# Two mixture-of-experts stages: results scattered back per expert, weights loaded during the layernorm, a rewritten routing chain

## What is computed

```python
x = x + attn_a(layernorm(x))
x = x + ffn(layernorm(x))
x = x + attn_b(layernorm(x))
x = x + ffn(layernorm(x))

# ffn: E = 8 experts, capacity C = 2048 / 8 = 256 tokens each
logits = einsum('gtd,de->gte', xt, router_w)
probs = softmax(logits); gate = max(probs); idx = argmax(probs)
emask = one_hot(idx, E)
pos = cumsum(emask, axis=1) * emask - 1          # place of the token within its expert
dispatch = emask[..., None] * one_hot(pos, C)    # a token past the capacity is dropped
h = relu(einsum('gecd,edf->gecf', expert_inputs, w1) + b1)   # 128 -> 512
y = einsum('gecf,efd->gecd', h, w2) + b2                     # 512 -> 128
out = einsum('gecd,gtec->gtd', y, dispatch * gate)
```

## Time and profile before

| | |
|---|---|
| median of 3 runs | 1302.0 us (1299.88 to 1302.25) |
| the profiled execution, its own time | 1302.2 us |
| its span, first to last instruction | 1300.6 us |
| mean granted TensorE clock | 0.884 |
| busy: PE, weight load, DVE, ACT, POOL | 79%, 51%, 60%, 46%, 26% |
| first expert stage, statistics to last addition | 607.8 to 720.8 us |
| second expert stage, same | 1183.1 to 1293.1 us |

### The profile page before, as it was taken

How to read it: one execution, slowest core, us unless ns; L and a number is a source line. 1 busy time by engine, 2 the same in 40 slices (tenths; PEclk the granted TensorE clock), 3 DMA queues, 4 the chain that set the end, 5 groups by cost and what they waited for, 6 DMA issues and landing times. The chain is left out here.

```text
span 1300.6 us, 19242 instructions
## 1 busy us (share of the span) xinstructions
PE 1033.4 (79%) x6462; PEld 661.4 (51%) x6462; DVE 782.7 (60%) x1948; ACT 596.9 (46%) x1155; POOL 341.5 (26%) x451
## 2 busy tenths in 40 slices
PE   3499999999999999997263427879999999985180
PEld 2357666666666666664253326445544445434080
DVE  5166756766676657775212696787777777736031
ACT  2366656666666656663020300542555555563020
POOL 0421112111211022100324100773443334320504
PEclk9589999999999999998577756877999999996595
DMA  5500000000000000000142000000000000000252
GB/s 177 131 1 2 1 1 1 1 1 1 1 1 1 1 1 2 1 1 1 58 129 81 7 0 1 1 1 1 1 2 1 1 2 1 1 1 1 85 153 69
DMA packets 40028, 30.05 MB, mean 23 GB/s; under 512 B 9200, under 2 KB 35584, under 8 KB 39936
## 3 DMA queue, kind: packets, MB, share of 16 engines
q1 hardware_dynamic: 35392, 19.43, 5.4%
q0 software_dynamic: 2816, 6.30, 1.6%
q10 hardware_dynamic: 1728, 3.15, 0.8%
HBM read 21.50 MB, written 9.46 MB: 24 GB/s over the span
## 5 line engine op out<-in xcount | busy, mean ns | idle before, releaser
L709 DVE TENSOR_REDUCE attn_b_least<-attn_b_slot 128x1 f32<-128x512 f32 (+3 forms) x384 | 195.1, 553 | 62.2 <-PE attn_b_slot L627 42.0
L440 ACT ACTIVATE attn_a_prob<-attn_a_score,attn_a_m_all 128x128 f32<-128x128 f32 (+7 forms) x256 | 189.1, 739 | 74.6 <-DVE attn_a_m_all L362 70.3
L776 ACT ACTIVATE attn_b_probT<-attn_b_st 128x1024 f32<-128x1024 f32 (+1 forms) x192 | 145.2, 808 | 149.9 <-PE attn_b_st L651 148.6
L358 DVE TENSOR_REDUCE attn_a_m_far<-attn_a_score 128x1 f32<-128x512 f32 (+3 forms) x192 | 105.8, 551 | 95.3 <-PE attn_a_score L272 91.3
L296 PE MATMUL attn_a_o<-attn_a_ptsb,Vd 128*64 128x512 f32 x288 | 156.1, 624 | 0.0
L296 PE MATMUL attn_a_o<-attn_a_ptsa,Vd 128*64 128x512 f32 x288 | 156.0, 624 | 0.0
L284 PE MATMUL attn_a_slot<-tab,attn_a_prob 128*128 128x128 f32 x1152 | 150.2, 274 | 0.0
L625 PE MATMUL attn_b_slot<-KS,attn_b_alone 128*128 128x512 f32 (+2 forms) x384 | 145.8, 448 | 4.5 <-POOL attn_b_alone L798 2.9
L284 PEld LDWEIGHTS attn_a_slot<-tab,attn_a_prob 128*128 128x128 f32 x1152 | 133.1, 142 | 11.1 <-issue 2.4
L625 PEld LDWEIGHTS attn_b_slot<-KS,attn_b_alone 128*128 128x128 f32 x384 | 73.6, 202 | 87.7 <-DVE attn_b_least L709 52.6
L449 ACT ACTIVATE attn_a_ptsa<-attn_a_slot 128x512 f32<-128x512 f32 x144 | 85.7, 595 | 60.9 <-PE attn_a_slot L284 60.4
(11 more groups left out here) (219 smaller groups left out, 1926.2 us busy)
## 6 DMA issues: line engine op xcount, KB each, us to landing
moe_experts_w<-in_L_ffn_w_dram SPq DMA_DIRECT2D x20, 256.0 KB, 2.8
moe_experts_w<-in_L_ffn_w_dram ACTq DMA_DIRECT2D x12, 256.0 KB, 3.6
bias_by_query_and_key<-bias_by_distance SPq DMA_DIRECT2D x2, 1024.0 KB
bias_near<-bias_by_query_and_key SPq DMA_DIRECT2D x2, 1024.0 KB, 8.2
moe_experts_xe<-to_experts POOLq DMA_DIRECT2D x16, 128.0 KB, 2.7
from_experts<-moe_experts_ye SPq DMA_DIRECT2D x16, 128.0 KB, 3.3
to_experts<-xn SPq DMA_DIRECT2D x1, 1024.0 KB, 5.4
from_experts<-xn SPq DMA_DIRECT2D x1, 1024.0 KB, 8.9
```

Source lines behind the costliest of these rows:

```text
L358: nc.vector.tensor_reduce(least, score[t % 2][:, 0:nk - win], AX.X, ALU.min).then_inc(far_done, 1)
L440: nc.scalar.activation(probs(g)[:, j, 0:nk], score[t % 2][:, 0:nk], ACT.Exp, bias=m_all[:, j:j + 1], scale=-1.0, accum_out=rowsum[g % 2][: ...
L709: nc.vector.tensor_reduce(least[m // PER % 2][:, c, a, qt:qt + 1], bank[u % SLOTS_S][:, 0:w], AX.X, ALU.min).then_inc(slot_free, 1)
L776: nc.scalar.activation(probT[n % 2][:, two, lo:], st[:, two, lo:], ACT.Exp, scale=-1.0).then_inc(exp_done, 1)
```

## The change

- `layernorm`: the router products of four tiles are issued between the turns, after the turns of the next four. `xn` gets a row of 132 numbers (`DW = D + 4`), of which number 128 holds the token's own index.
- `moe` opens the weights of all eight experts (`w1`, `w2`, `b2`: 36 KB a partition) before the layernorm, and SP issues their 24 loads in the layernorm's block.
- `route`: the expert is picked from the shifted logits, not from the exponentials; the gate is computed later in the chain; the eight scans become one over 128 elements that reads PSUM directly, with `fresh` set to zero where a new expert begins; several pairs of operations become one, and several links are gone. One more small operation writes the token's index into `xn`.
- `experts`: the scatter of `xn` carries the index along (rows of 528 bytes). SP, not POOL, loads each expert's rows, all eight at once, into their own places. After each expert's output POOL scatters its 256 rows straight to their token's row in the second DRAM buffer (two indirect transfers of 128 rows, with the indices that came with the input rows). When all have landed, SP loads the rows back in token order with four plain transfers of 256 KB. The output buffer `ye` (a ring of two) is written again only when its two scatters have landed (`returned`). Loops are unrolled. ACT copies expert 1 before the relu of expert 0; DVE does relu(e+1) before the output addition of e.
- The buffers exist once for each `moe` call, so four are cleared beside the first attention, not two. The first block gets one more DVE operation behind its last ones, and one memset in a wait.

```diff
 # layernorm, PE
+            def logits(g):
+                pe.wait_ge(copied, g + 1)
+                for i in range(g * BLK, (g + 1) * BLK):
+                    at = 1 + (i % QT) * P
+                    nc.tensor.matmul(logit[:, i, :], xnT[:, i // QT, at:at + P], router[:, :], start=True, stop=True)
             for i in range(TILES):
                 pe.wait_ge(xn_ready, i + 1)
                 j = i % BLK
-                ins = nc.tensor.transpose(bank[i // BLK][:, j * P:(j + 1) * P], xn[:, i, :], ident[:, :])
+                ins = nc.tensor.transpose(bank[i // BLK][:, j * P:(j + 1) * P], xn[:, i, 0:D], ident[:, :])
                 if j == BLK - 1:
                     ins.then_inc(turned, 1)
-            for i in range(TILES if router is not None else 0):
-                ...
+                    if router is not None and i >= BLK:
+                        logits(i // BLK - 1)
+            if router is not None:
+                logits(TILES // BLK - 1)
 # route, DVE
-            nc.vector.memset(one[:, :], 1.0)
+            nc.vector.memset(fresh[:, :, :], 1.0)
             link(nc.vector.tensor_reduce(m1[:, :], logit[:, :, :], AX.X, ALU.max))
-            ... L949 to L978
+            nc.vector.tensor_tensor(rank[:, :, :], logit[:, :, :], wide(m1), ALU.subtract).then_inc(shifted, 1)
+            nc.vector.tensor_scalar(token, spare[:, :], -(SLOTS + 1.0), None, ALU.add)
+            dve.wait_ge(shifted, 1)
+            link(nc.vector.scalar_tensor_tensor(best[:, :, :], rank[:, :, :], 0.0, prio[:, :, :], ALU.is_equal, ALU.mult))
+            link(nc.vector.tensor_reduce(m2[:, :], best[:, :, :], AX.X, ALU.max))
+            nc.vector.tensor_tensor(mask_bf[:, :, :], best[:, :, :], wide(m2), ALU.is_equal).then_inc(masked, 1)
+            nc.vector.tensor_tensor(mask[:, :, :], best[:, :, :], wide(m2), ALU.is_equal)
+            link(nc.vector.memset(fresh[:, :, 0:1], 0.0))
+            link(nc.vector.tensor_tensor(base[:, :, :], mask[:, :, :], ebase[:, :, :], ALU.mult))
+            link(nc.vector.tensor_reduce(first_row[:, :], base[:, :, :], AX.X, ALU.add))
+            link(nc.vector.tensor_tensor(first_row[:, :], first_row[:, :], spare[:, :], ALU.subtract))
+            dve.wait_ge(exped, 1)
+            nc.vector.tensor_reduce(m3[:, :], ex[:, :, :], AX.X, ALU.max)
+            link(nc.vector.tensor_reduce(m4[:, :], ex[:, :, :], AX.X, ALU.add))
+            link(nc.vector.reciprocal(m5[:, :], m4[:, :]))
+            nc.vector.tensor_tensor(gate[:, :], m3[:, :], m5[:, :], ALU.mult)
+            dve.wait_ge(counted, 1)
+            link(nc.vector.tensor_tensor_scan(run[:, :, :].rearrange("p e t -> p (e t)"), fresh[:, :, :].rearrange("p e t -> p (e t)"),
+                                              total, 0.0, ALU.mult, ALU.add))
+            dve.wait_ge(counted, 2)
+            ... subtract total, add count, times mask, sum, keep, row, times keep
+            nc.vector.scalar_tensor_tensor(slot[:, :], row[:, :], -1.0, spare[:, :], ALU.add, ALU.add)
 # experts, POOL after the scatters of xn
-            pool.wait_ge(sent, 16 * TILES)
-            ... rows of each expert, then the 16 gathers
+            for e in range(E):
+                pool.wait_ge(ye_ready, e + 1)
+                for c in range(2):
+                    token = xe[:, 2 * e + c, D:D + 1].bitcast(I32)
+                    pool.indirect_dma_start(out=ye_dram[:, :], out_offset=bass.IndirectOffsetOnAxis(ap=token, axis=0),
+                                            in_=ye[e % RING][:, c, :], in_offset=None).then_inc(returned[e % RING], 16)
 # experts, SP
+            sp.wait_ge(sent, 16 * TILES)
+            for e in range(E):
+                sp.dma_start(xe[:, 2 * e:2 * e + 2, :], bass.AP(tensor=xe_dram, offset=e * (CAP * DW),
+                                                                ap=[[DW, P], [P * DW, 2], [1, DW]])).then_inc(xe_ready[e], 16)
+            for i in range(RING):
+                sp.wait_ge(returned[i], 32 * (E // RING))
+            for i in range(TILES // BLK):
+                sp.dma_start(back[:, i * BLK:(i + 1) * BLK, :], bass.AP(tensor=ye_dram, offset=i * (BLK * P * D),
+                                                                       ap=[[D, P], [P * D, BLK], [1, D]])).then_inc(fetched[i], 16)
 # experts, ACT and DVE
+            copy(0)
+            copy(1)
+            relu(0)
+            for e in range(E):
+                if e + 1 < E:
+                    relu(e + 1)
+                if e + 2 < E:
+                    copy(e + 2)
 ...
+            relu(0)
+            for e in range(E):
+                if e + 1 < E:
+                    relu(e + 1)
+                dve.wait_ge(y_done, e + 1)
+                if e >= RING:
+                    dve.wait_ge(returned[e % RING], 32 * (e // RING))
+                nc.vector.tensor_tensor(ye[e % RING][:, :, :], y_ps[e % RING][:, :, :],
+                                        b2[:, e, :].unsqueeze(1).to_broadcast([P, 2, D]), ALU.add).then_inc(ye_ready, 1)
 # build, moe: SP, in the layernorm's block
+                        for e in range(E):
+                            sp.dma_start(w1[:, e, :], t["w1"][e]).then_inc(weights[e], 16)
+                            sp.dma_start(w2[:, e, :, :], t["w2"][e].rearrange("(f p) d -> p f d", p=P)).then_inc(weights[e], 16)
+                            sp.dma_start(b2[:, e, :], row(t["b2"], D, e * D)).then_inc(weights[e], 16)
 # build, first block, DVE, between the two bf16 copies
+            nc.vector.tensor_scalar(xn[:, :, D].bitcast(I32), col["spare"], -1.0, None, ALU.add)
```

More of the change, by code:

```diff
@@ L1150, in _, with relu @@
-            with dve.Fori(0, ITS) as it:
-                body(it)
+            def relu(e):
+                dve.wait_ge(h_done, 2 * e + 2)
+                if e >= RING:
+                    dve.wait_ge(y_done, e - RING + 1)
+                for f in range(2, FB):
+                    ins = nc.vector.tensor_scalar(hT[e % RING][:, f, :], h_ps[2 * (e % RING) + 1][:, f % 2, :],
+                                                  b1T[:, f, e:e + 1], 0.0, ALU.add, ALU.max)
+                ins.then_inc(relu_dve, 1)
```

277 lines of the change are left out of this document (97 added, 180 removed).

## The result

The changed kernel took 1258.5 us, the median of four runs (1256.5 to 1265.3), beside 1301.5 for the kernel before (1299.9 to 1302.3). The ratio is 0.968 (95% interval 0.964 to 0.972). The forecast was 1262.3. Timed a second time, the same pair gave 1263.8 and 1298.3, ratio 0.973 (0.970 to 0.976), so the gain is 35 to 43 us and is not known more closely than that. The profiled execution took 1256.5 (span 1254.7), 45.8 less than that of before.

What follows compares the result with a forecast made beforehand. It took the expert stages to be bound by serial scatters, landings, experts and gathers, with PE stalled by ACT and DVE order. Gains of 20.25 us per stage, twice 40.5, less 0.65, took 1302.2 to 1262.3; range 1255.5 to 1272.

Steps and rivals of the forecast that it cites:

- the return: Last expert output to last rows back: 24.1 us becomes 9.8, a gain of 14.3 per stage, bounds 12.0 to 15.3.
- the routing: Routing chain after the layernorm: 9.1 us becomes 6.5, a gain of 2.6 per stage, bounds 2.0 to 3.0.
- Waits for `returned`: Expert loop: output buffer waits for scatters two experts back; costs nothing while a scatter costs POOL under about twice 1.28 us.
- The rivals in which POOL binds: Expert loop: each scatter waits for the previous landing, 2.53 us each, 11.8 more per stage, 1286 us; chance 0.08.
- the slower one: Expert loop: scatters dearer than 3.04 us each make the kernel slower than before; at 3.3 and 0.3, 1320 us; chance 0.02.
- Order on ACT and DVE: Expert loop: copy(1) before relu(0) and relu(7) before ye(6) remove two PE stalls, 2.85 us per stage, bounds 2.0 to 2.9.
- Rows: Last scatter's landing to PE's first turn: 2.86 us becomes 2.35 with SP loading, a gain of 0.5 per stage.
- Router products: Layernorm: moving products between turns gains 0, as PE has no idle time there; bounds 3 us either way.
- Weights beside the layernorm: Layernorm block: SP's 24 weight issues take 11.6 us and end before PE's last product, costing 0.
- a sign of being wrong: Layernorm block: the forecast would be wrong if SP's last weight issue ended a layernorm block.
- the rival: Layernorm block: SP's weight issues hold its end, price 2.5 us, giving 1264.8; chance 0.13.
- Once: Costs once per kernel: 0.5 us for SP's extra semaphore clears before the final store, 0.15 for one DVE operation.

Runs made afterwards that it cites:

- the old way back: Changed kernel with SP storing each expert's rows and POOL gathering 16 tiles at the end, as before the change: 1286.0 us, ratio 0.992.
- the products last: Changed kernel with the router products issued after all layernorm turns, as before the change: 1258.7 us, ratio 0.970.
- the unread products of the experts block: Changed kernel plus sixteen 128x128 products that nobody reads, on PE once the twelfth scatter has landed: 1256.3 us, ratio 0.968.

## Why the prediction was right, and where it was not

**The sum.** The stages gave 38.7 us where the terms gave 40.5, and the medians 43.0 and 34.5 where the forecast said 39.9. The terms were right within 1 us each but for one, the second layernorm, and the errors had both signs: what this one lost (2.7 us), and what the return lost (0.9 a stage), the loop and the routing gave back in part (0.7 and 0.5 a stage). That they cancel so nearly is luck, and so is how near a single median comes to the forecast, with stretches outside the change moving by up to 7 us. What is not luck is the return, over two thirds of the sum, with the mechanism that was forecast.

**Return: mechanism right, one piece left out.** The last output to the last rows took 10.5 and 10.4 us in the two stages; I had 9.8. Inside it the pieces moved: 0.27 instead of 0.8 from the wait to a scatter; but the last output comes 1.8 us after the one before it, since no relu stands between them any more, and its scatters queue behind that pair, so that the first starts 1.0 after the output. The landing took 2.24, as assumed, so the scatters are 0.3 over in all. The four loads took 5.9 and 5.7 us from the first issue to the last landing (5.5 to 5.9 in six stages), against 5.5 assumed, which was nearer than either row, 5.0 or 6.7. The 6.15 us that the Trainium skill (DMA: Bandwidth & Descriptors, section Bandwidth) states for 1 MB are the transfer alone, measured for one issued from GpSimd; all six stages here took less, with issue and landing included. I also ended the sum at the last rows. Behind them DVE still has 1.5 us of additions, 0.3 more than before, because from the first landing on the 16 additions leave it hardly idle. Late rows (0.6) and the longer end (0.3) are the 0.9 by which the term missed.

**Waits for `returned` and POOL.** No idle time of DVE is put down to the scatters, they stand 1.27 apart and 0.97 long beside DVE's work, and the old way back left the loop unchanged. The rivals in which POOL binds, and the slower one, did not happen. The port rule of the Trainium skill (SBUF — State Buffer, section Who interferes with whom) had no price here; DVE's operations in the loop take one input from PSUM, so the loop is no test of operations with two inputs in SBUF.

**Order on ACT and DVE: sum right, owners wrong.** The loop gave 3.5 to 3.7 instead of 2.85. The order alone is worth about 2 of it (1.8 to 2.5), most of it at the end. The step that failed is "copy(1) ahead of relu(0) removes the stall": the profile's releaser of ACT's idle time was PE's hidden layer, which neither of these two needs, and which the queued load of `w1` did. I read who held PE (ACT) and did not read what held ACT.

**Rows.** The gain was 0.44 / 0.50, as said; the first rows landed 2.23 after SP's issue.

**Routing.** 6.0 instead of 6.5 and outside its bound of 6.1. The one scan took 0.41, between the estimate 0.34 and the bound 0.6; the rest is overlap: operations that aren't linked start before the one ahead has ended (1171.43, 1171.64 and 1171.76 in a row of 0.29, 0.17 and 0.29), and two maxima and a memset cost little beside others. I had added durations; unlinked operations are to be counted by their spacing.

**Router products: in the bounds, and not zero.** The forecast had no change in either stage. PE's last product came 0.5 us sooner in the first and 2.6 later in the second. The step that failed is taking the clock of the second stage as given: the rows showed that the turns ran at half speed and the products at full, and I took that as a matter of time and not of what PE had done before. "PE has no idle time that the products could fill" was wrong as well, by 0.5 us: turns that show as gapless were waiting for DVE.

**Weights beside the layernorm.** 24 issues took 13.9 and 13.8 us, not 11.6. The six in a row that I measured were the first of their block; from the twelfth issue on, the `b2` issues, of 0.5 us, took 0.7 to 1.4. In the second stage PE's slower block hid it; with the products last SP held that block by 0.3. In the first stage SP started 2.1 us after the statistics, behind the semaphores of the attention, and ended 16.0 to 16.8 after them, not near 13; the interleaved products ended at 16.0 too. So SP's last issue ended the first layernorm's block in all three profiles of the changed kernel, which the prediction had named as a sign of being wrong, and part or all of the 0.5 us that the interleaving gains there went to it. The step that failed is the price of an issue, taken from six; the rival was right about the mechanism and had the price too high (2.5; measured 0.2 to 0.9, in one stage).

**Once.** The final store was issued 0.37 later, 0.5 forecast.

## What to carry to other kernels

A term that ends in a transfer has to be followed to the last instruction that uses the data: when a slow producer goes, more of the consumer's own work stands behind the last landing. And a chain names the transfer that released something, which need not be the last of its group. When the profile says that PE waited for ACT, read ACT's queue too: an instruction that issues a transfer can hold the engine for a buffer, and moving the arithmetic around it repairs nothing. And where an engine's clock differs between two stretches of one trace, look whether the order of instructions does too: it went with the order here, and neither "busy" nor "busy without a gap" was enough to bring the clock up.

## What the runs showed of the hardware

The granted clock of TensorE rose from 0.50 to 1.00 after 3.6 to 4.0 us of turns alone in the second layernorm (three of three, and none of three in the first), 3.3 to 6.5 us into the expert loop of the changed kernel and its variants, and 3.6 to 6.2 us into the unread products of the experts block; it did not rise in 10.4 us of turns and eight-column products that PE's records show without a gap, in 16 stages of eight executions that had this order and no unread products ahead of it; the last product came 15.99 to 16.01 us after the statistics' start in all of them. The Trainium skill (TensorE: Matmul & The Clock Gate, Part 1) says that the default state is throttled and that activity releases it. The first cases agree with it; in the last PE's records have no gap, and the clock stayed at 0.50. A loop with the clock full from its start took 31.0 to 31.1 us in seven of eight stages and 31.3 in the other, against 32.4 to 34.0 where it had to rise.

An issue on SP is not of fixed price: mostly 0.43 and 0.51 us for `w` and `b2` among the first nine of a block of 24, and 0.9 to 1.9 for the longest of each block, most often the twelfth. And 256 KB of weights took 4.9 us to land where all 24 were queued, against 2.8 in the loop of the kernel before; no wait in either kernel ended on them.
